# Block results of a sorted mixture of experts scattered to their pairs' rows; eviction on ScalarE, half of the weights' lows on VectorE

## What is computed

```python
scores = softmax(xt @ router_w + router_b) + router_bias
# two of four groups, then the best two of the experts left: 2 experts a token
y  = sum over a token's 2 experts of gate * ((silu(xt @ w1 + b1) * (xt @ w2 + b2)) @ w3 + b3)
z  = silu(xt @ sw1 + sb1) * (xt @ sw2 + sb2) @ sw3 + sb3          # shared expert, twice as wide
x  = x + y + z
```

## Time and profile before

| | us |
|---|---|
| median of 3 runs | 608.86 (608.28 to 609.4) |
| the profiled execution: its time | 612.38 |
| the profiled execution: its span, first to last instruction | 610.6 |
| the block loop, from the third block's `up` to the shared expert's first product | 115.35 to 183.69 |
| from there to the first transpose that the query phase waits for | 183.69 to 218.47 |
| query phase, attention, output projection, bottleneck | 218.47 to 610.6 |

### The profile page before, as it was taken

The page is one execution under the profiler, slowest core; times in us unless marked ns, Lnnn a source line. Parts: engine busy times, 40 slices in busy tenths (PEclk is TensorE's granted clock), DMA queues, the critical chain, the costliest instruction groups (busy, mean ns, idle before and its releaser), DMA issues.

```text
span 610.6 us, 11610 instructions
## 1 busy us (share of the span) xinstructions
PE 562.1 (92%) x3232; PEld 273.6 (45%) x3232; DVE 408.7 (67%) x1049; ACT 345.2 (57%) x858; POOL 349.6 (57%) x371
## 2 busy tenths in 40 slices
PE   2999998798969989999868999999999999999997
PEld 0445444576644444444313444444444344444453
DVE  6898756494535965555689999999999900001782
ACT  4575866543432276777666777877777723142131
POOL 5993375788956237989844544445444534477011
PEclk9999999899989999999989999999999999999999
DMA  9996289999968206989599999999999984342001
GB/s 338 413 383 244 53 214 199 253 383 408 396 236 308 89 10 181 204 202 214 114 224 175 180 169 182 180 178 183 180 179 182 174 172 167 105 152 87 2 1 69
DMA packets 211622, 118.78 MB, mean 195 GB/s; under 512 B 188017, under 2 KB 196337, under 8 KB 208642
## 3 DMA queue, kind: packets, MB, share of 16 engines
q1 hardware_dynamic: 209122, 108.58, 70.6%
q0 software_dynamic: 2288, 9.70, 4.3%
q10 hardware_dynamic: 176, 0.04, 0.0%
HBM read 56.94 MB, written 15.20 MB: 118 GB/s over the span
## 4 chain that ended last, share of the span: by engine, by line
PE 39%; POOL 19%; DVE 13%; issue 11%; SPq 8%; DMA 5%; ACT 4%; DVEq 0%; POOLq 0%; ACTq 0%
PE ps L358 12%; PE ps L360 11%; PE ps L359 11%; SPq L513 8%; POOL hlr L1317 5%; POOL wsp L1317 5%; POOL q_sb L1317 3%; PE ps L667 2%; PE ps L540 2%; POOL xs_dram L1358 1%; POOL pT L1317 1%; POOL q_sb L1334 1%; DMA stage<-in_moe,disp 1%; DMA wsp<-hlr 1%; POOL q_sb L1430 1%
## 5 line engine op out<-in xcount | busy, mean ns | idle before, releaser
L1188 ACT ACTIVATE f32r<-f32r,mneg 128x512 f32<-128x512 f32 x128 | 91.5, 715 | 29.0 <-DVE mneg L1895 29.0
L1317 POOL TENSOR_TENSOR wsp<-stage,wsp 128x512 f16<-128x512 f32 (+1 forms) x69 | 78.4, 1166 | 49.0 <-ACT wsp L1159 44.1
L1895 DVE CUSTOM_DVE_ANT_0 f32r<-ps,nmask 128x512 f32<-128x512 f32 x128 | 82.4, 680 | 1.5
L1453 POOL TENSOR_SCALAR hlr<-f32r,rinv 128x512 f16<-128x512 f32 x64 | 44.8, 708 | 48.9 <-DVE rinv L1900 45.1
L1453 POOL TENSOR_SCALAR stage<-f32r,rinv 128x512 f16<-128x512 f32 x64 | 43.6, 691 | 47.5 <-DVE rinv L1900 42.9
L1317 POOL TENSOR_TENSOR hlr<-f32r,hlr 128x512 f16<-128x512 f32 x36 | 41.3, 1158 | 44.5 <-ACT hlr L1269 33.6
L358 PE MATMUL ps<-q_sb 128*128 128x512 f16 x132 | 50.7, 384 | 14.6 <-POOL q_sb L1317 12.0
L358 PE MATMUL ps<-k_sb,q_sb 128*128 (+1 forms) x128 | 49.5, 387 | 11.7 <-DVE mneg L1895 8.9
L1905 DVE SCALAR_TENSOR_TENSOR hlr<-f32r,rinv,hlr 128x512 f16<-128x512 f32 x64 | 50.1, 818 | 1.3 <-POOL hlr L1453 1.3
L1905 DVE SCALAR_TENSOR_TENSOR stage<-f32r,rinv,stage 128x512 f16<-128x512 f32 x64 | 49.2, 807 | 2.3 <-POOL stage L1453 2.3
L360 PE MATMUL ps<-q_sb 128*128 128x512 f16 x132 | 50.5, 383 | 0.0
(11 more groups left out here) (365 smaller groups left out, 1427.1 us busy)
## 6 DMA issues: line engine op xcount, KB each, us to landing
stage<-in_wq SPq DMA_DIRECT2D x8, 1024.0 KB, 6.1
stage<-in_wo SPq DMA_DIRECT2D x8, 1024.0 KB, 4.8
q_sb<-in_moe SPq DMA_DIRECT2D x9, 768.0 KB, 9.1
xs_dram<-zeros SPq DMA_DIRECT2D x1, 5888.0 KB, 28.8
pT<-xs_dram SPq DMA_DIRECT2D x23, 256.0 KB, 7.5
r_dram<-f32r SPq DMA_DIRECT2D x23, 256.0 KB, 7.0
k_sb<-in_wkv SPq DMA_DIRECT2D x3, 1024.0 KB, 18.8
stage<-in_moe SPq DMA_DIRECT2D x4, 768.0 KB, 10.1
```

Source lines behind the costliest of these rows:

```text
L1188: act.activation(f32r[:, j % 4, :], f32r[:, j % 4, :], ACT.Exp, bias=mneg[:, j % 4:j % 4 + 1], scale=-1.0, accum_out=psum_col[:, j % 4:j % ...
L1317: return pool.tensor_tensor(dst_lo, src, dst_hi, ALU.subtract)
L1453: pool.tensor_scalar(halves(j)[:, 0, :], f32r[:, j % 4, :], rinv[:, 0, j % 4:j % 4 + 1], PSCALE, ALU.mult, ALU.mult).then_inc(s_ph, 1)
L1895: dve.tensor_tensor_reduce(f32r[:, j % 4, :], ps[j % 4][:, :], nmask[:, qt, :], 0.125, BIG, ALU.add, ALU.min, mneg[:, j % 4:j % 4 + 1]).th ...
```

## The change

- `r_dram` has one row for each pair (1024) and no longer one for each slot. POOL writes a block's result by an indirect DMA (`scatter_result`) whose index says for each of the 128 lanes which pair's row it is; an empty slot has an index beyond the bounds and is left out.
- Those indices are made beside the keys: DVE builds one-hot tiles of lane and block (`rows_of_slots`), in rounds 8 and 11, PE multiplies them by 8 small products (`rows_of_blocks`) in rounds 12 and 15, DVE turns the sums into indices (`rows_counted`) in round 15.
- `evict` moves from DVE to ACT, between `silu(n)` and `w12_hi(n + 2)`. With it moves its wait for the landing of the buffer three blocks earlier.
- From block 2 on, POOL does the low half for the first 512 columns only; DVE does the second 512 (`w12_lo` on DVE, a new semaphore `s_w12d` that PE waits for).
- In POOL's iteration the order is `scatter_result(n - 2)`, gathers, `w12_lo(n + 2)`.
- The final collection of the pairs' rows is now eight plain loads on SP's queue in place of eight gathers on POOL's. They stand behind the load of the first query weights and in front of the second.

```diff
-    r_dram = nc.dram_tensor("r_dram", (SLOTS, D), F32, kind="Internal").ap()
+    r_dram = nc.dram_tensor("r_dram", (2 * TOK, D), F32, kind="Internal").ap()
 # SP
-                if n >= 2:
-                    store_result(n - 2)
-            store_result(NB - 2)
-            store_result(NB - 1)
+            sp.wait_ge(s_re, NB)
             load(0, wq[0], WG)
+            for n in range(3):
+                sp.wait_ge(s_rst[n], 16 * ((NB - n + 2) // 3))
+            for t in range(NT):
+                for k in range(2):
+                    if 2 * t + k == 5:
+                        sp.wait_ge(s_w3l, 2)
+                        sp.wait_ge(s_w12l, ALL)
+                        sp.wait_ge(s_w12d, ALL - 2)
+                    sp.dma_start(got[t][k], r_dram[(k * NT + t) * P:(k * NT + t + 1) * P, :]).then_inc(s_got[t], 16)
             load(1, wq[1], WG)
 # PE, up(n) and shared_up(n)
+                if n >= 2:
+                    pe.wait_ge(s_w12d, n - 1)
 # PE, rounds 12 and 15 of the keys
+            def rows_of_blocks(k):
+                pe.wait_ge(s_idx, 2 + k)
+                for t in range(NT):
+                    last = pe.matmul(ps[7][:, 0:NB], at_lane[t], at_block[t], start=(k == 0 and t == 0),
+                                     stop=(k == 1 and t == NT - 1), skip_group_check=True)
+                last.then_inc(s_pos, 1)
 # ACT
+            def evict(n):
+                act.wait_ge(s_dn, n + 1)
+                if n >= 3:
+                    act.wait_ge(s_rst[n % 3], 16 * (n // 3))
+                act.copy(f32r[:, n % 3, :], ps[n % 4][:, :]).then_inc(s_re, 1)
             for n in range(1, NB):
                 silu(n)
+                if n >= 2:
+                    evict(n - 2)
                 w12_hi(n + 2)
+            evict(NB - 2)
+            evict(NB - 1)
 # POOL
-                for u in range(2):
+                for u in range(2 if n < 2 else 1):
+            def scatter_result(n):
+                pool.wait_ge(s_re, n + 1)
+                pool.indirect_dma_start(r_dram, bass.IndirectOffsetOnAxis(ap=row_of[:, n:n + 1], axis=0), f32r[:, n % 3, :], None,
+                                        bounds_check=2 * TOK - 1, oob_is_err=False).then_inc(s_rst[n % 3], 16)
             for n in range(NB):
-                w12_lo(n + 2)
+                if n >= 2:
+                    scatter_result(n - 2)
                 for m in range(E_ROUTED, NB):
                     if BEFORE[m] == n - 2:
                         gather_expert(m)
+                w12_lo(n + 2)
+            scatter_result(NB - 2)
+            scatter_result(NB - 1)
-            (eight gathers of got from r_dram)
 # DVE
+            def rows_of_slots(k):
+                own = slice(k * NT, (k + 1) * NT)
+                if k == 0:
+                    slot = disp[:, 0:2 * NT].bitcast(I32)
+                    dve.wait_ge(s_idx, 1)
+                    dve.tensor_scalar(pair, number[:, 0:2 * NT], float(P), 1.0, ALU.mult, ALU.add)
+                    link(dve.tensor_scalar(block_int, slot, 7, None, ALU.arith_shift_right))
+                    dve.tensor_copy(block_of, block_int)
+                    dve.tensor_scalar(pair, pair, lane, None, ALU.add)
+                    link(dve.scalar_tensor_tensor(out=lane_of, in0=block_int, scalar=-float(P), in1=slot, op0=ALU.mult, op1=ALU.add))
+                else:
+                    dve.wait_ge(s_pos, 2)
+                for t in range(NT):
+                    at = k * NT + t
+                    dve.tensor_scalar(at_lane[t], lanes, lane_of[:, at:at + 1], None, ALU.is_equal)
+                    last = dve.tensor_scalar(at_block[t], lanes[:, 0:NB], block_of[:, at:at + 1], pair[:, at:at + 1],
+                                             ALU.is_equal, ALU.mult)
+                last.then_inc(s_idx, 1)
+            def rows_counted():
+                dve.wait_ge(s_pos, 3)
+                link(dve.tensor_scalar(unused, ps[7][:, 0:NB], 0.0, 65536.0, ALU.is_equal, ALU.mult))
+                dve.scalar_tensor_tensor(out=row_of, in0=unused, scalar=-1.0, in1=ps[7][:, 0:NB], op0=ALU.add, op1=ALU.add)\
+                   .then_inc(s_disp, 1)
+            def w12_lo(n):
+                at = slice(KC * INTER, 2 * KC * INTER)
+                dve.wait_ge(s_w12h, n + 1)
+                dve.tensor_tensor(split_at(n, 1, at), landed_at(n, at), split_at(n, 0, at), ALU.subtract).then_inc(s_w12d, 1)
             for n in range(NB):
                 if n + 1 < NB:
                     slots_turned(n + 1)
+                if n >= 1:
+                    w12_lo(n + 1)
                 gated(n)
-                if n >= 2:
-                    evict(n - 2)
```

52 lines of the change are left out of this document (26 added, 26 removed).

## The result

| | before | changed |
|---|---|---|
| median of the runs | 609.4 us | 615.76 us (613.95 to 618.04) |
| ratio, 95% interval | | 1.0105 (1.0062 to 1.0148) |
| profiled execution, its span | 612.38 us, 610.6 us | 618.04 us, 616.3 us |
| moved in all | 118.78 MB | 114.86 MB |
| `up(2)` to `up(10)` | 22.39 us | 29.25 us |

Slower by 1.05%, where 1.2% faster was forecast. A profiled execution can lie some us off its kernel's median: before's lies 3 above, the changed one's 2.3 above. The profiled executions of e11_order, e12_all and e13_tail were disturbed before and behind the blocks; lengths are read from them mainly within the blocks.

A forecast was written before the change was run, and what follows sets the result against it. PE paces the kernel, losing about 10 us in the block loop to waits on DVE, full queues and POOL. Loop -6.5, keys +0.4, tail -1.1 sum to -7.2 us: median 608.86 to 601.7, range 598.0 to 607.0.

The forecast's parts named there:

- Loop's start, keys: Before the block loop: `up(2)` no longer waits for a second low, -0.4; index work beside the keys, +0.4 us.
- Blocks 2 to 10: Early loop: blocks go at PE's pace, 8 x 2.70 = 21.6 us in place of 22.4, -0.8.
- Part 3: ACT and DVE: ACT has room for evictions; DVE swaps a 0.7 us copy for a 0.68 subtraction, costing nothing.
- PE's own block hides it: DVE's low, held by POOL's, ends at 2.0 to 2.6 us, before `up(n + 1)` at 2.70; uncovered, up to 0.96 a block.
- Blocks 10 to 22: Later loop, with POOL slower than PE in gather iterations: 37.5 us in place of 41.56, -4.1.
- The first rival: POOL slower in iterations 10 to 18, by held lows or 1.22 us scatters: gain 2 to 5 us; chance 0.20.
- The gather's landing: Last weights' gather before `up(22)`: 5.8 us to land, between 4.2 and 7.43.
- `up(22)` to the shared expert: End of the loop: 3.2 us in place of 4.4, -1.2, if PE barely idles in front of it.
- Tail: Behind the blocks: eight plain loads replace gathers, shortening DVE's chain before the query's transposes, -1.1 us.
- Part 3's ring: Scatter, landing and eviction span three blocks: at least (landing + 0.7)/3 a block, 1.6 us at 4.2; few rows cost nothing.
- Part 1: DMA queues: result rows fall from 2944 to 1024, 3.9 MB less; full up to about block 10, room behind it.
- The third rival: Slower: scatter holds POOL far longer, gain gone at 1.54 us, 618 at 2.0; chance 0.09.

The follow-up runs named there:

- e11_order: Changed kernel, with ACT evicting behind its high halves and POOL scattering behind its gather and low: 611.25 us, ratio 1.0039.
- e12_all: Changed kernel with the edits of e11_order, e7_mended and e13_tail together: 610.45 us, ratio 1.0010.
- e13_tail: Changed kernel, with DVE's second shared gate and its low half ahead of the first addition of read-back results: 616.83 us, ratio 1.0111.
- e1_psum: Changed kernel, with DVE's w2 low in blocks 2 to 23 replaced by an equally long PSUM read writing zeros: 610.11 us, ratio 1.0002.
- e2_late: Changed kernel, with DVE's three pieces of small work moved from iterations 4, 6, 8 to 19, 13, 17: 610.92 us, ratio 1.0022.
- e16_scatter_behind: Changed kernel, with POOL scattering behind its gather and low, ACT's order kept: 614.97 us, ratio 1.0083.
- e9_pool_lows: Changed kernel, with both halves of the lows on POOL again: 624.72 us, ratio 1.0243.
- e14_both: e12_all, with DVE making both low halves for the seven blocks of gather iterations and owners' biases moved to iteration 15: 608.59 us, ratio 0.9974.
- e5_half: Kernel before, with DVE making the second half of the lows from block 2: 610.29 us, ratio 1.0016.
- e7_mended: e5_half, with owners' biases moved to iteration 13, small lows to 19, pairs' gates behind the blocks: 610.94 us, ratio 1.0004.
- e15_thin: e7_mended, with only a quarter of each block result's columns stored, gathered and added: 602.83 us, ratio 0.9871.
- e17_four: e14_both, with four eviction buffers in turn instead of three: 608.95 us, ratio 0.9978.
- e4_evict: Kernel before, with the eviction on ACT ahead of its high halves: 615.23 us, ratio 1.0089.
- e8_dve_evict: Changed kernel, with the eviction back on DVE: 622.76 us, ratio 1.0218.

## Why the prediction was wrong

The forecast was 601.7 (598.0 to 607.0), faster with 0.88. By its own terms:

- **Loop's start, keys: right.** `up(2)` at 115.33, forecast 115.35 - 0.4 + 0.4.
- **Blocks 2 to 10: -0.8 forecast, +6.9 measured. This is the step that failed.** Part 3 has the held low hidden: it "ends at 2.0 to 2.6, before `up(n + 1)` at 2.70". For a block without small work that is right: the low of 118.91 takes 1.69 us and ends 2.57 behind `up(3)`. The row it took the price from, 123.24, is a hold behind one low of GpSimd. Here the low starts inside a scatter and is held through that and the low behind, 2.39 instead of 1.64, and the small work's own two-input instructions are held as well (132.21). In iterations 4, 6 and 8 all this adds up on one in-order engine, and the low's lateness stops PE. e1_psum, e2_late and e16_scatter_behind each take one part of it away, and A falls to 24.00, 22.24 and 23.34. "PE's own block hides it" is true of a block without small work (e2_late) and was not summed for the three with it. The kernel before already showed 0.59 of idle PE at `up(10)`, which the prediction blamed on small work and an eviction; it took the eviction's 0.7 out and put a low in, as an even exchange.
- **The clock on top.** After the stops of 2.47 and 2.48 us PE's granted clock is 0.50, the lower of its two levels, 1.2 GHz, for some 3.5 us each; 24 products then take 2.72 us instead of 1.50. The prediction had this for `up(22)` alone.
- **Blocks 10 to 22: -4.1 forecast, -0.7 measured.** GpSimd's iteration was put at 3.62 and is 3.90. The scatter is 1.27 and not the 0.97 "since gathers of three times the bytes cost the same as scatters", because it meets VectorE's low; e9_pool_lows and e1_psum have 1.00. A further 1.7 is the lowered clock behind `up(10)`. The first rival had a scatter longer by 0.25, the right size, but gave it to the check of bounds, and held lows on GpSimd besides, where one of 1.65 was seen (183.69). It came out 9 us too low at the least, because it looked for the loss in iterations 10 to 18 only. The gather's landing, 5.8 forecast, was 5.4 in the median, with some luck: in e14_both, whose queues are not emptied by stops, it is 6.5 to 7.4.
- **`up(22)` to the shared expert: right,** 3.12 for 3.2.
- **Tail: -1.1 forecast, +1.6 measured.** The step "now it waits for no gather" priced the loads from a last scatter 2.1 us behind the shared product; it started 3.7 behind, and the first load landed at 201.04. No row shows the 7.3 us from the last landing to the last load; the eight loads were issued from 197.13 to 200.7 and took 4.2 us in the median to land. VectorE's last addition ends 20.0 us behind the first shared product, where the kernel before has 18.5: that is the loss. That VectorE's second shared gate stands behind the landing was not seen, but the 616.83 of e13_tail say that it costs nothing.
- **Part 3's ring was right, its queue was not.** Scatters land in 4.0 us and ScalarE waits for none. But GpSimd's order, eviction, scatter, low, was not looked at for what it does to VectorE: the scatter and the low behind it stand back to back at just the time of VectorE's low. e16_scatter_behind undoes this. GpSimd's scatter also waits for the eviction, 12.9 us in six waits, but all of these fall before 152 us, where PE's stops name VectorE; that they cost anything by themselves isn't shown.
- **Part 1 right.** "the queues stay full up to about block 10 and have room behind it": the DMA share is 1.00 from 137 to 144.5, `up(10)` is at 144.58, and from 150 to 165 there are 278 GB/s where before had 394. But the change lets nothing use this room. In reverse, e5_half and e7_mended free GpSimd without making room, and gain nothing either; e15_thin has both and is 7 us faster than before, 1.1 of it in D.

The third rival (slower) asked for a long scatter. It was an in-order queue instead: the changed kernel's scatters take at most 1.38, and the loss in blocks 2 to 10 is on VectorE. What the medians of e5_half, e7_mended and e12_all lose against the sums of their best stages is not fully accounted for. Full transfers may explain the first two. For the kernels with scatters a part is the tail. With scatters VectorE's last addition ends 19.7 to 21.5 us behind the shared expert's first product, and D is 36.0 to 37.9; with whole blocks stored it ends at 18.2 to 19.2, and D is 34.6 to 35.5. So e17_four gains 5.1 us on the kernel before in A to C, 1.3 of them the lower clock in before's C, and gives 1.9 back in D. A stretch at the lower clock also falls into the shared expert's products in many profiled executions (e1_psum, e2_late, e4_evict, e7_mended, e9_pool_lows, e14_both): the last `down` then begins 17.4 us behind the first product instead of 15.7. In e1_psum and e2_late PE still waits 1.56 and 1.75 us for VectorE at the end of D, so it costs little there. Why it comes in some kernels and not in others stays open, and so does the rest.

## What to carry to other kernels

Before work is moved to an engine, write out that engine's in-order queue for the worst iteration, with everything else that it does there, and take the longest hold that its neighbour's back-to-back instructions can cause, not that of one. Of two instructions in a queue, put the one that others wait for ahead of the one that may wait: swapping the eviction with the high halves turned +5.4 us into nothing, and that swap together with one on GpSimd brought 4.5 of the 6.4 us of this change back. And where a stage has two limits close together, here GpSimd and the transfers, taking away one can show nothing until the other goes too.

## What was not expected of the hardware

- VectorE's instruction with two SBUF inputs (0.68 us) that starts 0.36 to 0.64 us into a scatter's issue is held until GpSimd's next low has ended as well, 2.11 and 2.39 us; it is not let in between the two. One that starts 0.20 us into a scatter (135.76, scatter at 135.56) runs in 0.68. A scatter that starts while such a low runs takes 1.26 to 1.38 us in the changed kernel instead of 1.00 (163.23, with VectorE's low from 162.75 to 163.63). The Trainium skill, SBUF — State Buffer, Who interferes with whom, infers that a tensor_tensor doesn't stand in the way of descriptor generation, because it takes only the read interface. The trace differs for these indirect DMAs: VectorE's instruction with two inputs and the scatter lengthen each other (132.21, 163.23).
- Leaving rows out of a scatter by an index out of bounds costs GpSimd nothing (1.00 us) and shortens the landing, 4.0 us in the median against 6.4 with all rows written.
- A stop of PE of 2.47 and one of 2.48 us were followed by the lower clock in the changed kernel, but one of 2.47 in e2_late (before `up(21)`) and one of 3.15 in e8_dve_evict (before `up(22)`) were not; no length of stop in these runs decides it. Each such stretch costs about 1.7 us of a PE-bound stage, more than many an edit here.
